# The third layer's bias: eighty bias products on TensorE, or four GpSimd additions a group

## The reference, cut to what matters

```
def _L2_gnn_ref(h, adj, W, a, bias):
    Wh = jnp.einsum('bnf,fo->bno', h, W)
    f1 = Wh @ a1
    f2 = Wh @ a2
    e = jax.nn.leaky_relu(f1[:, :, None] + f2[:, None, :], negative_slope=ALPHA)
    e = jnp.where(adj[None, :, :] > 0, e, NEG_INF)
    attention = jax.nn.softmax(e, axis=2)
    h_prime = jnp.einsum('bij,bjo->bio', attention, Wh) + bias
    return jax.nn.elu(h_prime)

h = jnp.maximum(_layernorm(x, axis=-1), 0.0)
x = x + _L2_gnn_ref(h, adj, L2_gnn_W, L2_gnn_a, L2_gnn_bias)
```

## Time and profile before

| | us |
|---|---|
| median of 3 runs | 975.24 (973.69 to 977.46) |
| the profiled execution's own time | 974.64 |
| its span, first to last instruction | 972.9 |

### The profile page before, as it was taken

One profiled execution on the slowest core, in us unless ns is written; L12 is line 12 of the kernel. 1 busy time (PEld: TensorE's weight loads), 2 busy tenths in 40 slices (PEclk: granted clock), 3 DMA queues, 4 the chain that ended last, 5 costly groups with the idle time before them and its releaser, 6 DMA issues. The chain is left out here.

```text
span 972.9 us, 21043 instructions
## 1 busy us (share of the span) xinstructions
PE 911.1 (94%) x7051; PEld 859.5 (88%) x7051; DVE 834.1 (86%) x2593; ACT 757.8 (78%) x2048; POOL 440.0 (45%) x1123
## 2 busy tenths in 40 slices
PE   4968899999999899999999999999999999989997
PEld 3858798999988899999989899998999998988896
DVE  5788899999986889988989898789999888889873
ACT  4798678878778884986798887998868888678863
POOL 6734257334546522552474433644345445445330
PEclk8989999999999999999999999999999999999999
DMA  5200000000020010011000101101000100000004
GB/s 138 66 2 3 1 2 1 2 1 2 16 73 2 2 45 1 2 44 45 2 1 2 44 1 45 44 2 44 2 2 1 45 1 2 1 1 2 1 1 130
DMA packets 43052, 20.05 MB, mean 21 GB/s; under 512 B 8248, under 2 KB 42432, under 8 KB 42944
## 3 DMA queue, kind: packets, MB, share of 16 engines
q1 hardware_dynamic: 41056, 18.49, 7.0%
q10 hardware_dynamic: 1888, 0.21, 0.2%
HBM read 10.17 MB, written 8.39 MB: 19 GB/s over the span
## 5 line engine op out<-in xcount | busy, mean ns | idle before, releaser
L728 PE MATMUL ps<-HE,PT 128*128 128x129 f32 x2048 | 239.5, 276 | 4.8 <-issue 2.6
L728 PEld LDWEIGHTS ps<-HE,PT 128*128 128x128 f32 x2048 | 233.2, 192 | 7.6 <-issue 5.5
L497 ACT ACTIVATE Y<-X,SM 128x128 f32<-128x128 f32 x512 | 204.0, 493 | 16.5 <-POOL SM L493 15.9
L478 POOL TENSOR_TENSOR SM<-ST 128x8 f32<-128x8 f32 x96 | 32.6, 340 | 392.1 <-DVE ST L1289 392.1
L1429 DVE SCALAR_TENSOR_TENSOR PT<-ps,CE,maskT 128x512 f32<-128x512 f32 x256 | 174.2, 743 | 14.7 <-PE ps L842 10.9
L489 POOL TENSOR_TENSOR SM<-SM,minus_half 128x8 f32<-128x8 f32 x96 | 167.5, 1744 | 7.6
L728 PE MATMUL ps<-W,HT 128*128 128x128 f32 x768 | 117.3, 276 | 0.7 <-DVE MX L1407 0.5
L728 PEld LDWEIGHTS ps<-W,HT 128*128 128x128 f32 x768 | 106.5, 192 | 4.8 <-issue 1.8
L1289 DVE BATCH_NORM_STATS2 ST<-X 128x6 f32<-128x128 f32 x512 | 105.0, 278 | 6.4 <-DMA X<-in_x_dram 2.5
L746 PE MATMUL ps<-ident,Y 128*128 128x128 f32 x512 | 66.4, 275 | 8.9 <-ACT Y L497 8.8
L1064 ACT ACTIVATE HE<-ps,HE 128x128 f32<-128x128 f32 x256 | 69.1, 382 | 0.0
(11 more groups left out here) (265 smaller groups left out, 2280.9 us busy)
## 6 DMA issues: line engine op xcount, KB each, us to landing
X<-in_x_dram SPq DMA_DIRECT2D x32, 256.0 KB, 3.4
out_dram<-X SPq DMA_DIRECT2D x32, 256.0 KB, 2.8
adj_raw<-in_adj_dram SPq DMA_DIRECT2D x4, 256.0 KB, 3.8
UP<-US SPq DMA_DIRECT2D x64, 2.0 KB, 1.8
W<-in_L_gnn_W_dram SPq DMA_DIRECT2D x2, 64.0 KB, 3.8
W<-in_L_gnn_W_dram SPq DMA_DIRECT2D x1, 128.0 KB, 3.5
feat0w<-L_gnn_others_weight_dram ACTq DMA_DIRECT2D x1, 64.0 KB, 3.3
feat1w<-in_L_gnn_Wp_dram ACTq DMA_DIRECT2D x1, 64.0 KB, 3.7
```

Of the source, the lines that this page charges most:

```text
L478: TT(sm[:, S_DIF, :], st[:, :, 1], st[:, :, 4], ALU.subtract)
L497: a = nc.scalar.activation(dst[:, n, 0:F], src[:, n, 0:F], func, scale=SM[s][:, S_RSTD, n:n + 1], bias=SM[s][:, S_SHIFT, n:n + 1])
L728: return nc.tensor.matmul(o, w, m, start=start, stop=stop, skip_group_check=True)
```

## The change

- `feat2` loses its bias products: the two `feat2w` products of a tile now open it themselves. `sums2` loses its one too. `bias_q`, `bias_n`, their filling in the set-up (two memsets, one L550, two L553 on POOL, one L627 on ACT) and two of ACT's DMAs (the third bias into `brow`) go away.
- `bias2`, the bias in all 128 partitions, is loaded by one more DMA on SP's queue.
- A new POOL step `base2` waits for `by_act` and adds `bias2` to the base rows in `HT[s]` with four instructions of 128x256, in place, two SBUF inputs each. It raises `added`, and `elu2a/b` wait for that instead of `by_act`.
- `TURNS` and `HOMES` are new for all engines: of PE's 454 turns 256 keep their relative order.

```
--- before.py
+++ after.py
@@ STEPS
     ("sums2", 1, "pe act"),
+    ("base2", 0, "pool"),
     ("top2", 1, "pe dve act"),
@@ TURNS["pool"], first line
-    "pool": ("g0152431002134g01203510412502342165734623467878536845979a696a57897a6b87b8abcd9a89cdabcedeb9cebdfafcd"
+    "pool": ("g1024031502413g05120310412500121324653724623467384357846589796a589765a796a7b687b8abcd98a89dcba9ecd9e"
...
@@ set-up
-                for zeros in (pick, bias_p, bias_q, bias_n, bias_1, bias_2):
+                for zeros in (pick, bias_p, bias_1, bias_2):
...
-                for k, bias in enumerate((bias_p, bias_1, bias_2, bias_q)):
+                for k, bias in enumerate((bias_p, bias_1, bias_2)):
                     link(TT(bias[32:33, 0:F], brow[32:33, k, :], bhi[32:33, k, :].bitcast(F32), ALU.subtract))
                 pool.wait_ge(made["bhi"], 2)
-                for p0 in (0, 32):
-                    link(TS(bias_n[p0:p0 + 1, :], bias_q[p0:p0 + 1, 0:F].bitcast(F32), float(N), None, ALU.mult))
@@ PE, sums2
                     o, done = open_tile(u, "sums2", s)
-                    MM(o[:, 0:G * P], pick[:], repeat(bias_n[:], G), True, False)
                     for b in range(G):
-                        mm = MM(o[:, b * P:(b + 1) * P], wide(HS[s][:, b, 0:1]), feat2w[:, 0:F], False, True)
+                        mm = MM(o[:, b * P:(b + 1) * P], wide(HS[s][:, b, 0:1]), feat2w[:, 0:F], True, True)
@@ PE, feat2
-                    "feat2": lambda u, s: feat(u, "feat2", s, feat2w[:], bias_q, "norm2"),
+                    "feat2": lambda u, s: feat(u, "feat2", s, feat2w[:], None, "norm2"),
@@ POOL
+                def base2(u, s):
+
+                    pool.wait_ge(sig["by_act"][s], count(u.g, 3, 1))
+                    m = HT[s][:].rearrange("p b n -> p (b n)").rearrange("p (t b f) -> p t b f", t=T, b=G)
+                    for t in range(T):
+                        a = TT(m[:, t], m[:, t], repeat(bias2[:], G), ALU.add)
+                    a.then_inc(sig["added"][s], 1)
@@ DVE
                 def elud2(u, s, b):
-                    dve.wait_ge(sig["by_act"][s], count(u.g, 3, 1))
+                    dve.wait_ge(sig["added"][s], count(u.g, 1, 0))
```

More of the change, by code:

```diff
@@ new lines @@
+    "dve": ("120ggg54g0g10023g01g012g0140004121341110035200352201141105301222331015433423124004232534531125355001"
+           "1002024040011523501151144220103453614152423726246226226336642247666573735237433784374636377578464864"
+           "834468578875838438776978868859474997569a998999575a6655a599a596796785a89a6a55aaa76b766766aa877a7a67b7"
+           "9bb86b87ab7b6b9bba7a8c89db88ba8888db9c9dbac8c8adbc9d9c8c9ccec9ba9add9dbde9da9cecebaeccaaeecdee9de9db"
+           "b9cdeecfedaeabfbcdfdfbefbfffdffbabeccffeffdbcfcbcdffecacadfdeeddcdffdebecdcefedeefceeffbbffeffddfeec"
+           "cdff"),
@@ new lines @@
+    "pool": ("g1024031502413g05120310412500121324653724623467384357846589796a589765a796a7b687b8abcd98a89dcba9ecd9e"
+           "bacebfdcfabedfcfcdebfedfecdfef"),
+    "sp": ("1354001224350617672883994aa5bb6c7ddc8ee9ffabcedf"),
+}
+HOMES = ("0123456701234567012345671025673410256173402561730425173042510462735107346521052731460527314631052761"
+         "2743610527436106105621743054346201573420157616342034571625734160250723416435070251647303250325164703"
+         "2541767032451673205173621736052173460521734605260260517342651703426517043276045160327324516073247234"
+         "5167034214521454267103542354671203547163540271563271324056565716571632405713205671467320514051673232"
+         "3672367232764075132076451320513726451307264531050315072642364231507641230764507235076471762345016274"
+         "3574301627451632745104527102450637150632471506473215321523064740767406715243015243015261453026174531"
+         "7453026174671465302746523703170707465230741652304165716572304130472657120346534653465712065347206515"
+         "3472067215306724674674267426153072164215364215073642361507402361572401536723640157231530153726401641"
+         "065347213406572134065450645067213415341530672306572413065417265416572")
@@ L337, in gnn_kernel @@
             "permuted", "result", "stored", "var", "rstd", "normed", "extent", "hi", "lo", "range", "dexp", "by_act",
-            "by_pool", "gated")}
+            "by_pool", "added", "gated")}
         weigh_order = sem("weigh_order")
@@ L466, in gnn_kernel @@
         VECTORS = [(brow[p0:p0 + 1, k, :], v.partition_broadcast(1)) for p0 in (0, 32)
-                   for k, v in enumerate((bp_d, b1_d, b2_d, bias2_d))] + [
+                   for k, v in enumerate((bp_d, b1_d, b2_d))] + [
                    (epscol[:], eps_d.partition_broadcast(P)),
@@ L1249, in coefp0 @@
                     TT(SM[s][:, S_B, :], SM[s][:, S_B, :], empty8[:], ALU.add).then_inc(sig["by_pool"][s], 1)
+                def base2(u, s):
[4 more added lines that the diff above has]
+                    a.then_inc(sig["added"][s], 1)
                 run = {
-                    "egin": egin, "elow": elow, "coefp0": coefp0,
+                    "egin": egin, "elow": elow, "coefp0": coefp0, "base2": base2,
                     "stat0": lambda u, s: rstd(u, "norm0", s),
```

52 lines of the change are left out of this document (17 added, 35 removed).

## The result

The changed kernel takes 980.72 us (median of 6 runs, 979.17 to 985.16); before takes 976.35 beside it (6 runs, 973.69 to 978.88). The ratio is **1.0045, 95% interval 1.0024 to 1.0065**: slower by 4.4 us, where 967.0 (959.5 to 975.5) was forecast. That is just inside the prediction's bound of 0.5% (4.9 us), slower by the interval, and clearly not faster.

A forecast was written before the change was run, and what follows sets the result against it. PE was taken to bound the kernel from 120 to 900 us. Products -9.6, set-up -1.2, POOL delays +1.1, SBUF contention +1.1 and order +1.0 gave -7.6 on 974.6: 967.0 us, range 959.5 to 975.5.

The forecast's parts named there:

- The premise: From 120 to 900 us PE is the bound, 97% busy, so work taken from it shortens the run by nearly its size.
- bias products: PE's 80 products in `feat2` and `sums2`, 0.12 us each: removing them saves 9.6 us.
- set-up: POOL ends its set-up over 1 us sooner and ACT issues two DMAs fewer: -1.2 us.
- passes' duration: POOL's new 128x256 passes in `base2` take about 0.73 us each, 46.5 us for all 64.
- What they delay on POOL: Passes delay POOL's queued scales that ACT waits for, and PE's waits at that chain's end grow by an eighth: +1.1 us.
- POOL against DVE in SBUF: Passes meet DVE's two-input instructions for about 11 us; DVE bears half, a fifth of it on the path: +1.1 us.
- order: New order of all engines: 0 within 4 us either side, plus a tenth of the saving lost to waits, +1.0 us.
- The first rival: The new order pays it back: 5 to 9 us of new PE waits in the middle, 973 us; chance 0.22.
- The third: DVE is blocked by POOL's passes, slower if 22 of 64 count in full: 982 to 987, say 984 us; chance 0.08.

The follow-up runs named there:

- the old order: Order strings and HOMES of before; the change run in them took 978.91 us (1.002), and without bias products and passes 975.52 us (0.997).
- with writes: Kernel before, products kept, with four GpSimd writes of zeros to a scratch tile a group where passes would run: 979.2 us, ratio 1.0005.
- the zero passes: Kernel before in its own order, all bias products kept, with four GpSimd passes a group added that add zeros: 982.57 us, ratio 1.0048.
- the passes under `att2a`: The change in the order of before, each group's passes held until DVE has ended its first instruction of `att2a`: 979.4 us, ratio 1.0027.

## Why the prediction was wrong

**The premise failed.** The step is "in four fifths of the run PE is the bound ... Work taken from PE there should shorten the run by nearly its own size". PE's 755 of 780 us busy is the time that its records cover, whose ends are modelled, and a high share does not say that PE's work sets the pace. Measured, 9.6 us of products and 1.2 of set-up are worth 2.9 us in the old order, the same products doubled cost 3.5, and 30 us of products are worth 9.3: 0.2 to 0.36 a us of PE in the old order, and 0.4 to 0.5 in the new, where the sum used 1. Three expectations above use shares of a chain of waits followed through the whole run (0.29 for PE, 0.25 for ACT, 0.39 for DVE). They are my own working, no view shows them, and they come out far apart with the way in which a wait is followed, so nothing rests on them here; the measured prices don't follow them either (0.08 for ACT; 0.13 down and 0.6 up for DVE).

**Term by term**, at the same clock. The *bias products* and the *set-up*: -9.6 and -1.2 predicted; together -2.9 in the old order and -5.2 in the new. The duration behind the first was about right (a tile takes 0.465 us where it took 0.57, so 0.10 us a product where 0.12 was read), the weight was not. The set-up did end 1.2 us sooner in the mean of the traces; what of it reaches the end of the run was not tried. The *passes' duration*: 0.73 predicted, 0.742 measured. *What they delay on POOL*: +1.1 predicted, +0.6 measured with writes, right within the errors; that it would come through PE's wait for ACT's scaled rows was not borne out in after, where this wait fell. *POOL against DVE in SBUF*: +1.1 predicted. The mechanism was the right one, and its size on DVE was somewhat short (5.5 us; 4.6, 7.0 and 9.2 measured, each against the same kernel without passes). The Trainium skill's rule (SBUF — State Buffer, Who interferes with whom), that whichever of the two issued first blocks the other, held in the direction that no row of before had shown, where the text left it open. What failed is "in its 87 us of spare time; a fifth of it on the path": less the hold the passes cost 4.2 to 4.5 us, which is 0.9, 0.6 and 0.5 for each of these us. The *order*: +1.0 with 4 to either side; +0.5 between the two kernels without passes and products, +0.8 with passes, +2.8 with the products kept, and by the measured ratios, with the clock that goes with the order, 2.9, 2.4 and 6.6.

With the parts as measured the sum is -2.9 + 4.8 + 0.5 = +2.4 us, the hold being within the 4.8, beside +2.7 measured. The parts add up, though they were measured after the fact. At the same clock the miss is 2.7 + 7.6 = 10.3 us: 7.9 in the products and the set-up (10.8 predicted, 2.9 measured), 2.6 in the passes (2.2 predicted, 4.8 measured), and 0.5 the other way in the order. By the prediction's own 967 the miss is 13.7 us: 1.4 more go with the lower clock, and before measured 1.7 us more beside the change (976.35) than the 974.6 that the sum started from.

**Of the rivals**, the first (new waits take the saved time's place, 973) came nearest to what became of the products: 2.9 of 10.8 us arrived. It put this down to DVE and ACT setting the pace, which the runs bear out for work added to DVE (0.6) and not for ACT (0.08), and it was laid aside with "DVE's spare time is nine times the saving". The third had the right mechanism with too high a bar: not 22 passes in full were needed, since the saving it had to outweigh was 2.9 us and not 10.8. Its mark, "DVE's 128x1024 instructions at 1.5 us or more where a pass runs", showed once (L1582 at 923.39); `elu2a` never waited. The first rival's mark, PE's waits at 30 us or more, showed at 33.9, and at 30.2 without passes.

**Open.** Why DVE is worth 0.13 a us when work is removed and 0.6 when it is added. A reading that would fit is that a written-out order fits the durations it was made for, so that every engine arrives just in time: an engine made faster then meets the others' waits, and one made slower meets them all late. For PE such a difference is not clear (0.36 doubled, 0.18 to 0.30 removed), and no order was made anew for any variant, so it is not shown. Also open is the 1.4 us between the 3.4 that DVE's lost time and the hold explain and the 4.8 that the zero passes cost: the price of a held-up us differed from 0.5 to 0.9 between kernels. And open is why the granted clock differs among the variants in the old order (0.980 to 0.988 in the mean of their runs), and what the new order's lower clock would cost by itself.

## What to carry to other kernels

A busy share of 97% on an engine is no proof that its work is on the path when the other engines stand at 80 to 90% and wait for each other in turn: price a us of each engine once, by doubling and by removing a harmless instruction, before an edit trades one against another. Moving work to an idle GpSimd is not free when it reads SBUF: the price is not GpSimd's time but what it takes from VectorE, so count it in VectorE's us, and at VectorE's price for added work (0.5 to 1 here, by place). Compare a variant with its own kernel without the one part, and look at what else the edit takes along: here a shorter set-up hid in the price of the products, and a lower clock in that of the order. A hold of GpSimd of the same length without reads cost 0.6 us here, and with reads 4.8.

## What was not expected of the hardware

- A VectorE instruction of only four columns, with one SBUF tensor and a scalar by pointer (L1418), is held by a GpSimd pass as a large one is: eight of 64 took about 0.765 us instead of 0.23. The size of an instruction does not protect it.
- Where both engines had a row of instructions, each one met the next: beside four passes, 528.8 to 531.8 us, four of L1366 took 0.81 to 0.82 us instead of 0.345, and the passes 0.77 to 0.83 us instead of 0.728. The four of L1366 ahead of them took 0.34 to 0.35 us.
- GpSimd's memset of 128x756 (0.729 us a piece, 46.7 us in all) left VectorE's total as it was, 834.2 us against 834.1.
- Runs of one kernel differed by up to 8.6 us with their granted clock: 975.31 us at 0.991 and 983.95 at 0.977 for the passes under `att2a`.
